# Scan and attention output of layer 0 in one program, with the products ahead of the next turn's transposes

## What is computed

```
out = outs.transpose(1, 0, 3, 2, 4).reshape(Bb, Ll, dm)      # from the 32 scan steps
out = _ln(out, post_w, post_b, eps=1e-05)                    # first norm, 256 wide
return out @ wo                                              # 256 x 256
# and around it, in the layer:
#   y = layernorm(out @ wo) (ln_w, ln_b), then @ up_w + up_b, to width 128
#   x = x + that + the result of layer 0's other block (ffnT), then a layernorm for layer 1
```

## Time and profile before

| | us |
|---|---|
| median of 3 runs (lowest to highest) | 456.18 (453.63 to 457.63) |
| the profiled execution's own span | 454.2 |
| PE busy | 388.6 (86%) |
| DVE, ACT, POOL busy | 298.4, 295.7, 183.7 |

### The profile page before, as it was taken

One profiled execution on the slowest core, in us unless ns is written; L12 is line 12 of the kernel. 1 busy time (PEld: TensorE's weight loads), 2 busy tenths in 40 slices (PEclk: granted clock), 3 DMA queues, 4 the chain that ended last, 5 costly groups with the idle time before them and its releaser, 6 DMA issues. The chain is left out here.

```text
span 454.2 us, 10214 instructions
## 1 busy us (share of the span) xinstructions
PE 388.6 (86%) x3168; PEld 264.8 (58%) x3168; DVE 298.4 (66%) x1033; ACT 295.7 (65%) x722; POOL 183.7 (40%) x301
## 2 busy tenths in 40 slices
PE   1999998959999999999964999976698568797993
PEld 1544343438777777777752677652443154675983
DVE  4757539345767777777763378875879976365185
ACT  4778686554766777667743557654679963796634
POOL 1306738023878888888878113233000030000003
PEclk9999999988999999999995599995979978898998
DMA  8221233251121222222155100000000000000003
GB/s 238 28 83 36 77 99 103 79 166 38 49 72 52 66 69 69 52 64 69 52 157 149 28 1 0 2 0 1 0 1 1 1 6 19 1 1 0 1 1 92
DMA packets 33003, 22.99 MB, mean 51 GB/s; under 512 B 10046, under 2 KB 32716, under 8 KB 32972
## 3 DMA queue, kind: packets, MB, share of 16 engines
q1 hardware_dynamic: 31724, 22.54, 18.3%
q10 hardware_dynamic: 1248, 0.07, 0.2%
HBM read 13.13 MB, written 9.47 MB: 50 GB/s over the span
## 5 line engine op out<-in xcount | busy, mean ns | idle before, releaser
L967 ACT ACTIVATE win<-bank 128x384 f32<-128x384 f32 (+1 forms) x124 | 44.0, 410 | 10.6 <-PE bank L910 10.2
L479 PE MATMUL bank<-w,hT 128*128 128x385 f32 x128 | 45.4, 495 | 0.4 <-ACT stage L605 0.4
L888 PE MATMUL bank<-win,wst 128*32 128x128 f32 x1024 | 44.0, 283 | 1.3 <-ACT kd L962 1.3
L479 PEld LDWEIGHTS bank<-w,hT 128*128 128x128 f32 x128 | 23.2, 189 | 24.5 <-issue 11.4
L1239 ACT ACTIVATE std_<-mv_,cst 128x2 f32<-128x2 f32 (+1 forms) x46 | 13.5, 296 | 31.8 <-DVE mv_ L1217 16.4
L888 PEld LDWEIGHTS bank<-win,wst 128*32 128x32 f32 x1024 | 26.5, 110 | 9.2 <-ACT kd L962 1.5
L1464 POOL TENSOR_TENSOR win<-win,lng 128x512 f32<-128x512 f32 x2 | 2.5, 1270 | 71.2 <-ACT win L1749 71.2
L1034 POOL TENSOR_SCALAR xh<-raw,bmv,brs 128x128 f32<-128x128 f32 x32 | 25.4, 793 | 2.6 <-DVE brs L1086 2.5
L1189 POOL TENSOR_TENSOR xn<-xn,out_b 128x128 f32<-128x128 f32 x16 | 7.3, 453 | 46.8 <-ACT xn1T L1255 46.8
L877 PE MATMUL bank<-win,cst 128*128 128x128 f32 x128 | 25.1, 278 | 0.9 <-ACT raw L988 0.9
L1027 POOL TENSOR_TENSOR xkm<-win,wst 128x256 f32<-128x256 f32 x32 | 19.6, 613 | 13.8 <-PE bank L910 6.9
(11 more groups left out here) (305 smaller groups left out, 1168.5 us busy)
## 6 DMA issues: line engine op xcount, KB each, us to landing
rows_scratch<-stage SPq DMA_DIRECT2D x32, 192.5 KB
win<-rows_scratch SPq DMA_DIRECT2D x32, 192.5 KB, 2.4
attn_scratch<-ob SPq DMA_DIRECT2D x32, 64.0 KB
att<-attn_scratch SPq DMA_DIRECT2D x4, 512.0 KB, 4.1
xt<-in_L_attn_x SPq DMA_DIRECT2D x4, 256.0 KB, 4.4
out<-win SPq DMA_DIRECT2D x4, 256.0 KB, 2.4
cst<-in_constants SPq DMA_DIRECT2D x1, 408.0 KB, 5.2
w<-in_L_attn_wk SPq DMA_DIRECT2D x2, 128.0 KB, 4.3
```

The costliest lines, as they stand in the source:

```text
L479: mm = nc.tensor.matmul(rows_bank(i, h)[:, 0:RC], hT[:, k, i * P:(i + 1) * P], w4[:, k, h, :], start=(k == 0), stop=(k == 1))
L888: mm = nc.tensor.matmul(dst[32 * b:32 * b + 32, 0:F], v[:, at:at + 2 * K], w_sb[:, state, first_slot(b) + h, :], start=False, stop=(h == 1 ...
L967: nc.scalar.activation(w_sb[:, state, at:at + n, :], bank[b][:, 0:n * F].rearrange("f (h g) -> f h g", h=n), ACT.Copy).then_inc(w_done, 1)
```

## The change

`ttt` and `layer0_out` no longer open a block of their own. They return their five engine programs (`Programs`), and `build` puts the scan's and the output's one behind the other in a single block, so there is no barrier between them. Three more things are changed.

1. Turn 0 of the output stands inside the end of the scan: on DVE between the last two `zbar` chains, on ACT ahead of the last `zbar_deviation`. POOL waits for the scan's last products, gradient and output before it clears the buffers that the scan used (`left`).
2. On PE the loop body is `products(n)`, then `turned(n)`: P(n) ahead of T(n), where T(n) was ahead of P(n).
3. The `wo` products rotate over banks 2, 3 and 7 in place of 2 and 3, `xn1` is turned in bank 6 alone, and a semaphore `h_read` of its own counts DVE's reads of the `up` products, for which PE now waits. `products(n)` also waits for the norms up to turn n - 2.

```diff
-            ttt(nc, a, locals())
-            layer0_out(nc, a, locals())
+            scan = ttt(nc, a, locals(), until_layer1)
+            tail = layer0_out(nc, a, locals(), until_layer1)
+            with nc.Block() as block:
+                @block.sync
+                def _(sp):
+                    scan.sync(sp)
+                    tail.sync(sp)
+
+                @block.tensor
+                def _(pe):
+                    scan.tensor(pe)
+                    tail.tensor(pe)
+
+                @block.scalar
+                def _(act):
+                    scan.scalar(act, lambda: tail.scalar(act, range(0, 1)))
+                    tail.scalar(act, range(1, tail.turns))
+
+                @block.gpsimd
+                def _(pool):
+                    scan.gpsimd(pool)
+                    scan.left(pool)
+                    tail.gpsimd(pool)
+
+                @block.vector
+                def _(dve):
+                    scan.vector(dve, lambda: tail.vector(dve, range(0, 1)))
+                    tail.vector(dve, range(1, tail.turns))
...
+        run_steps(act, step)
+        between()
+        zbar_deviation(STEPS - 1)
...
+                zbar_variance(t - 1, (p - 1) % RING)
+                zbar_scale(t - 1)
+                between()
+                zbar_variance(t, p)
+                zbar_scale(t)
...
+    def left(pool):
+
+        pool.wait_ge(zbar_mm, STEPS)
+        pool.wait_ge(grad_done, STEPS)
+        pool.wait_ge(ob_done, STEPS)
...
+    y_bank = lambda n: bank[(2, 3, 7)[n % 3]]
...
+        def products(n):
+
+            p = n % 2
+            if n >= 2:
+                pe.wait_ge(cp_done, n - 1)
+                pe.wait_ge(act_norms, min(n - 1, NT) + max(0, min(n - 4, NT)))
+            if n >= 7:
+                pe.wait_ge(h_read, min(n - 6, NT))
...
+        def turned(n):
+
+            p = n % 2
+            pe.wait_ge(act_norms, min(n, NT) + max(0, min(n - 3, NT)))
+            if n >= 7:
+                pe.wait_ge(norm_done, n - 6)
...
+        for n in range(1, TURNS):
+            products(n)
+            turned(n)
```

More of the change, by code:

```diff
@@ L756, in run_steps, with ttt @@
         step(STEPS - RING + p, p, left=RING - 1 - p)
-def ttt(nc, a, g):
+def ttt(nc, a, g, c):
     sb, sem, con, bank = g["sb"], g["sem"], g["con"], g["bank"]
@@ new lines, in ttt, with sync, flat, load @@
+    cc_done, xkm_done, xqb_done, ob_done = (sem(n, c) for n in ("cc_done", "xkm_done", "xqb_done", "ob_done"))
+    gd_done, xg_done, rr_done = sem("gd_done", c), sem("xg_done", c), sem("rr_done", c)
+    v_order, waited = sem("v_order", c), sem("waited", c)
+    MARKS = 7
+    def sync(sp):
+        def flat(v):
+            if len(v.shape) == 5:
+                return v.rearrange("t b h j c -> (t b h j) c")
+            return v.rearrange("b h j c -> (b h j) c")
+        at = lambda v, t: flat(v[t] if isinstance(t, int) else v[bass.ds(t, 1)])
+        def load(s, p):
+            if isinstance(s, int) and s == RING:
+                for parity in range(2):
+                    sp.wait_ge(m0.stored[parity], 32 * (NT // 2))
+            for used in (tr_mm, rr_done, xqb_done, xkm_done, gd_done):
+                wait(sp, used, s - RING + 1)
+            sp.dma_start(rows[:, p, :], at(rows_d, s)[:, 0:RC]).then_inc(rows_in[p], 16)
+        def store(t, p):
+            sp.wait_ge(ob_done, t + 1)
+            to = attn_d[t:t + 1] if isinstance(t, int) else attn_d[bass.ds(t, 1)]
+            sp.dma_start(to.rearrange("t k b h f -> b h (t k) f"), ob[:, p % 2, :]).then_inc(ob_out[p % 2], 16)
+        def step(t, p, left=RING):
+            if left >= RING:
+                load(t + RING, p)
+            if not (isinstance(t, int) and t == 0):
+                store(t - 1, (p - 1) % RING)
+            if 0 < left < TPB:
+                if left == TPB - 1:
+                    for parity in range(2):
+                        sp.wait_ge(ob_out[parity], 16 * (STEPS - P // K) // 2)
+                g["load_quarter"](sp, TPB - 1 - left)
+        run_steps(sp, step)
+        store(STEPS - 1, RING - 1)
@@ new lines, in layer0_out, with sync, gpsimd @@
+    rs_done, norm_done, tr_mm, cp_done, mm_done = (sem(n, c) for n in ("rs_d", "norm_d", "tr_d", "cp_d", "mm_d"))
+    h_read = sem("h_read", c)
+    marks = [0]
+    y_bank = lambda n: bank[(2, 3, 7)[n % 3]]
+    TURNS = NT + 7
+    LAST_SUM = NT + 4
+    on = lambda n, s: 0 <= n - s < NT
+    def sync(sp):
+        for p in range(2):
+            sp.wait_ge(g["ob_out"][p], 16 * STEPS // 2)
+        g["load_quarter"](sp, TPB - 1)
+        m1.load(sp, a)
+    def gpsimd(pool):
+        m1.clear(nc)
+        pool.wait_ge(m1.w_in, 16 * m1.loads)
+        for n in range(7, TURNS):
+            i = tile(n - 7)
+            pool.wait_ge(cp_done, n)
+            nc.gpsimd.tensor_tensor(xn1[:, i, :], xn1[:, i, :], m1.out_b[:], ALU.add)
+            nc.gpsimd.tensor_tensor(xt[:, i, :], xt[:, i, :], m1.lnb[:], ALU.add)
@@ L1313 @@
+    return Programs(sync, tensor, scalar, gpsimd, vector, turns=TURNS)
 class Layer1:
```

837 lines of the change are left out of this document (382 added, 455 removed).

## The result

The changed kernel takes 460.73 us (median of 4 runs, 459.91 to 461.9), the kernel before 455.28 (453.63 to 457.63) beside it on the same chip. The ratio on record is 1.0144, with a 95% interval of 1.0089 to 1.02, so the changed kernel is slower, by 1.4%. The prediction was 463.3 us, slower. The profiled execution spans 460.1 us, against 454.2 before.

A forecast was written before the change was run, and what follows sets the result against it. The prediction took PE to bound the output stage after the barrier's 7.20 us idle. Terms -6.0 + 2.0 + 0.6 + 8.5 + 2.0 = +7.1 us on 456.18 gave 463.3 us, range 455 to 473.

The forecast's parts named there:

- Term 1: From the scan's end to P(2): without the barrier, P(2) starts at 239.5 instead of 245.47, -6.0 us.
- Term 2: Output turns 2 to 5 at half clock: PE gets four waits for copies, 2.4, less 0.4 for T(2) replacing T(6), +2.0 us.
- Term 3: Output turn 6: +0.6 us if P(5)'s dense products bring full clock back as before, +2.9 if not back.
- Term 4: P(7) to P(17) at full clock: ten turns of 4.02 in place of 3.17 us, +8.5 us.
- 3.06 + 0.89 + 0.07: A full-clock output turn: PE's own work, exposed copies with signals, and lost overlap with T's end, 4.02 us.
- Term 5: The output's last turns: five turns from P(17) to T(22) where four followed T(18), +2.0 us.
- The clock stays up at the join: Shorter PE gaps after the scan keep turns 2 to 5 at full clock: 456.8 us, no change; chance 0.13.
- The thin turns lose the clock: PE's 0.9 us wait per output turn drops the clock, 2.4 us per turn hit: 475 to 487 us; chance 0.12.
- The hole isn't exposed: Copies finish before PE reaches P(n), so output turns take PE's own 3.06 us: 451 us; chance 0.07.
- A little more from the join, a little less from the holes: Output turns 0.15 us better each and clock back early, in turn 4 or 5: 457 to 460.5 us; chance 0.12.
- the forecast's own 460.5 to 468: Whole kernel: the main forecast's own range around 463.3 us, given a chance of 0.56.

The follow-up runs named there:

- after again: The changed kernel run once more, unchanged, for a second profile: 461.04 us.
- join alone: The changed kernel with PE's old order, T(n) ahead of P(n), and the old banks; joined block and turn 0 inside the scan stay: 450.13 us.
- order alone: The kernel before with only the new PE order and its banks; two blocks, the barrier between them, turn 0 behind it: 465.01 us.
- the kernel with the filled hole: The changed kernel with P(n)'s two matmuls that need no copies (bias row, ffnT) put ahead of the wait for the copies: 448.03 us.
- the run with fillers: The changed kernel with three unused 128x512 matmuls added on PE, two ahead of T(1), one after it: median 455.86 us; only the shortest run was profiled.
- those with the filled hole: The changed kernel with bias row and ffnT matmuls ahead of the wait for copies, plus three unused 128x512 matmuls around T(1): 441.47 us.

## Why the prediction was right, and where it wasn't

The distances between starts, in us, that the rows above and those of before give. The last two columns are the kernels with one half of the change each.

| | before | predicted | after | after again | join alone | order alone |
|---|---|---|---|---|---|---|
| scan's end to P(2) | 9.64 | 3.67 | 3.68 | 3.68 | 5.36 | 8.37 |
| P(2) to P(6) | 16.88 | 18.9 | 16.67 | 19.00 | 16.88 | 19.16 |
| P(6) to P(7) | 3.17 | 3.8 | 3.61 | 3.61 | 4.95 | 5.76 |
| P(7) to P(17) | 31.68 | 40.2 | 38.86 | 38.86 | 31.86 | 38.87 |
| P(17) to T(22) | 13.34 | 15.3 | 15.25 | 15.25 | 12.72 | 15.25 |
| scan's end to layer 1 | 76.96 | 84.1 | 80.11 | 82.45 | 73.80 | 89.44 |

**Term 1, the join, -6.0: right** (-5.96). The rows came where they were put: T(1) 1.9 us after the scan's end (1.8 predicted), and P(2) waiting 1.35 us behind it for ACT's copy (1.4 predicted). Two small errors cancelled: the parts named for P(2), 237.0 + 1.2 + 0.78 + 0.7, add up to 239.7 and not to the 239.5 used, and the last two of them took 1.20 us for 1.48. The last `zbar` root starts 1.99 us after the scan's end where it was 1.02, so what hangs on it moved by the predicted microsecond, and neither the output's turns nor layer 1's length shows it. POOL begins its clearing 4.70 us after the scan's end (4.96 before), far ahead of layer 1.

**Term 2, turns 2 to 5, +2.0: right in one profile, not in the other** (+2.1 and -0.2). The holes are there in both (0.47 and 0.75 us for the predicted 0.45 and 0.73). What differs is the turn in which the clock comes back: 0.83 already in 254 to 256 us of the first, and 0.54 in 256 to 258, 1.00 in 258 to 260 of the second, whose scan ends 2.5 us earlier. The prediction had this among its rivals, and said that its place moves the stage by 2 to 3 us. It could not say in which turn, so that +2.0 came out as +2.1 in one profile is in part luck.

**Term 3, turn 6, +0.6: right** (+0.44). The reason given for it, that the first dense products, P(5), bring the clock back, is not borne out: in the first profile the clock is up ahead of P(5) (P(5) starts at 255.50 with its bias row at 0.69), and with the order alone P(5) was over at 262.3 and the clock came back only at 268.5, behind P(6) too. There the turn was +2.6, near the upper bound of 2.9.

**Term 4, turns 7 to 17, +8.5: mis-sized, +7.2.** The mechanism is shown: the hole is 0.92 (0.89 predicted), it has ACT's copy as releaser ten times in ten, it is there with the barrier and without, it goes when the old order is put back, and filling it by 0.23 gives back 0.23. But a turn takes 3.89, not 4.02. The step that failed is "3.06 + 0.89 + 0.07". It took PE's own share of a turn to grow from 3.06 to 3.13, by the overlap that P loses to T's end. It shrinks to 2.97: T starts 0.16 before P's end (288.30 against 287.85 + 0.61 = 288.46), where the prediction had read 0.06, and T's first pair takes 0.38 where it took 0.44. From P's start to T's start is 2.26, T takes 0.71, and with the hole's 0.92 that is 3.89. Over ten turns the 0.13 are the 1.3 us by which the term was too large.

**Term 5, the drain, +2.0: right** (+1.91).

**Ahead of the scan's end** the first profile is 2.9 us late, of which nothing was predicted. It isn't the change's. The second profile of the same code is 0.4 late, and in the eight other experiments, whose work up to there is the same, the scan ends between 234.77 and 236.41. The same instructions, matched between the profiles, show where the 2.9 us arise. In layer 0's input one group of 128x512 matmuls takes longer. PE's timeline before:

```profile
11.60 2.78 PE L525 MATMUL bank<-xnT,down 128*128 128x512 f32 x4
```

and in the first profile of the changed kernel, with a wait further on that the kernel before does not have:

```profile
11.61 3.62 PE L551 MATMUL bank<-xnT,down 128*128 128x512 f32 x4
...
46.91 1.12 PE L522 MATMUL bank<-xn,cw 128*128 128x512 f32 x2 [1.01 <-DVE xn L473]
```

The later groups of the first kind take 1.88 us, so the longer ones look like half clock; the recorded clock has 1.00 there in the three profiles compared here and doesn't show it. By 18 us the first profile is 1.2 us behind. But the second profile has the same 3.62 us and is 1.0 behind by then, so the start alone doesn't make a late scan's end. The wait at 46.91, which neither other profile has, makes it 2.2, and by 98 us 2.35 (100.12 against 97.77). At the scan's beginning the clock falls in all three (0.50 in 102 to 104 us). In the second profile it is back in 104 to 106 us (0.94), and the delay is gone by 107; in the first it is still at 0.53 in 106 to 108, and the delay grows to 2.9. Why DVE was late at 46.91 in one profile stays open.

The delay of 2.9 us and the early clock in turn 5 happen to offset each other in the first profile (stage +3.15, ahead +2.9, layer 1 -0.2: +5.9); in the second the stage alone makes +5.5 of +5.7. Layer 1 takes 141.2 us against 141.4 before. The sum of +7.1 was too large by term 4's 1.3 us, and the medians differ by 5.5 and 6.2. Of the 2.6 us between the forecast's 463.3 and the measured 460.73, 0.9 are the level of the kernel before (456.18 in the forecast, 455.28 beside the changed kernel) and 1.7 the change.

**The rivals.** *The clock stays up at the join:* it fell, though PE's two gaps were 1.90 and 1.35 us. The windows with PE alone, first profile:

```profile
238.00:240.00 2.00, 0.76 (x16) 1.00 0.42 115
240.00:242.00 2.00, 0.44 (x2) 0.76 0.72 248
242.00:254.00 12.00, 10.62 (x24) 0.50 0.55 141
254.00:256.00 2.00, 1.25 (x6) 0.83 0.27 9
```

From 239 to 242 PE did one pair of transposes, and the clock fell at 241.0, as they ended. The second gap wasn't needed for the fall: in the second profile the clock fell inside the first gap, and so it did in the kernel with the filled hole, where no second gap follows. There PE idles from 235.61 to 237.50, and this window lies within:

```profile
237.00:237.20 0.20, 0.00 (x0) 0.50 1.06 358
```

With fillers, and gaps of 0.18 and 0.49 us, it stayed up, and P(2) to P(6) took 11.44 us, near this rival's 12.4. The fillers make the gaps shorter and PE busier at once, so which of the two held the clock isn't shown. The rival had the right price for an event that did not come. The Trainium skill, page "TensorE: Matmul & The Clock Gate", section "Why this matters for your kernels", warns of idle gaps of some microseconds; the run with fillers agrees, and the falls above came in or just behind a gap of 1.90 us, shorter than that.

*The thin turns lose the clock:* no. At 26.72 of 35 us busy it stays at 1.00, and at 15.45 of 20 in the run with the filler too. *The hole isn't exposed:* no, in every kernel where all of P waits for the copies. It is the filled version that does what this rival said: turns of 3.03 us against its 3.06. *A little more from the join, a little less from the holes:* half of it came. A turn was shorter than forecast by 0.13 us, and the clock was back early in one of two profiles. The time, 460.73, lies between this rival's 457 to 460.5 and the middle of the forecast's own 460.5 to 468, near where they meet.

Three things stay open: what decides in which turn the clock comes back, why DVE was late at 46.91 us in one profile, and why the filler with the holes left open gave runs that spread over 10 us and differ in their mean clock, where those with the filled hole spread over 2.

## What to carry to other kernels

Two edits that look like one can have opposite signs; here removing the barrier gave 4.7 us and the new order on PE took 10.9, so price them apart. On an engine that works in order, a product placed right behind the transposes it depends on pays in every turn for the signal to the copying engine, the copies and the signal back (0.92 us here), and either the next turn's transposes or a matmul that needs no copy belongs between; compare the length of what stands between with that of the copies. Where a bound engine is nearly empty for a moment before a stage with thin matmuls, look at the granted clock of the turns behind it, since a few matmuls without use in that moment can give more than the gap itself was worth: with the hole filled, 2.9 us of them gave 6.6. With the hole open their effect was not secured.

## What the runs showed of the hardware

- TensorE's full clock was lost at an idle time of only 1.90 us: in the first profile as T(1) ended (0.76 in 240 to 242 us, then 0.50), in the second and with the hole filled already inside the 1.90 us, 1.2 us after the scan's last product. With 2.9 us of matmuls in the same place it was held, in the profiled runs, for turns that kept PE busy only 15.45 of 20 us.
- At half clock, PE was busy in every 2 us window from 246 to 262 us of the kernel before, without a break, and the clock stayed at 0.50; in the first profile of the changed kernel it was busy 10.62 of 12 us at 0.50 and the clock rose after that. In all profiles where it fell at the join it came back between P(4) and P(7), at 253.9 to 268.5 us, and the same code differed by a turn.
- What comes ahead of the scan isn't equally long from one execution to the next. The scan's end, with the same instructions ahead of it, lay between 234.77 and 238.76 us, which is 0.9% of the span. A difference of this size in one profile's span says nothing until it is located.
